# Mixing the Fourier modes with one product over all 128 rows for both halves of the row frequencies, factors padded with zeros, and the scratch tensor of the modes laid out anew

## The reference

```python
x_ft = jnp.fft.rfft2(x)
out_ft = out_ft.at[:, :, :MODES, :MODES].set(jnp.einsum('bixy,ioxy->boxy', x_ft[:, :, :MODES, :MODES], w1))
out_ft = out_ft.at[:, :, -MODES:, :MODES].set(jnp.einsum('bixy,ioxy->boxy', x_ft[:, :, -MODES:, :MODES], w2))
return jnp.fft.irfft2(out_ft, s=(h, w))
```

## Time and profile before

| | us |
|---|---|
| median of 3 runs | 3841.19 (3837.57 to 3843.26) |
| profiled execution, time | 3846.3 |
| profiled execution, span of the trace | 3844.5 |
| TensorE busy in the span | 3672.3 (96%) |
| VectorE busy | 3525.7 (92%) |
| ScalarE busy | 3397.2 (88%) |
| mean granted TensorE clock, share of full | 0.984 |

### The profile page before, as it was taken

One profiled execution on the slowest core, in us unless ns is written; L12 is line 12 of the kernel. 1 busy time (PEld: TensorE's weight loads), 2 busy tenths in 40 slices (PEclk: granted clock), 3 DMA queues, 4 the chain that ended last, 5 costly groups with the idle time before them and its releaser, 6 DMA issues.

```text
span 3844.5 us, 103434 instructions
## 1 busy us (share of the span) xinstructions
PE 3672.3 (96%) x38186; PEld 1791.6 (47%) x38186; DVE 3525.7 (92%) x3959; ACT 3397.2 (88%) x3512; POOL 110.8 (3%) x132
## 2 busy tenths in 40 slices
PE   4995679999999999999999999999999999999998
PEld 2443334444444444444444444444444444444444
DVE  5773269999999999999999999999999999999997
ACT  1551269999999999999999999999999999999996
POOL 0000000000000000000000000000000000000000
PEclk9996899999999999999999999999999999999999
DMA  5999542332233223222322332232223223322321
GB/s 144 290 284 181 172 117 60 71 71 62 62 71 71 58 67 71 65 60 70 71 64 60 71 71 59 65 71 69 58 68 71 65 59 71 71 61 63 71 71 45
DMA packets 327345, 328.77 MB, mean 86 GB/s; under 512 B 87040, under 2 KB 259584, under 8 KB 325248
## 3 DMA queue, kind: packets, MB, share of 16 engines
q1 hardware_dynamic: 304256, 256.74, 24.9%
q0 software_dynamic: 18432, 67.12, 10.8%
q10 hardware_dynamic: 4608, 4.20, 0.3%
HBM read 239.90 MB, written 88.08 MB: 85 GB/s over the span
## 4 chain that ended last, share of the span: by engine, by line
PE 85%; DVE 0%; issue 0%; ACT 0%; POOL 0%; POOLq 0%; ACTq 0%; DVEq 0%
PE l_ps L1068 80%; PE y_ps L1055 3%; PE y_ps L1047 2%; DVE cube2l L944 0%; DVE cube3r L944 0%; ACT above L983 0%; ACT size L994 0%; ACT offset L998 0%; ACT S L987 0%; ACT below L991 0%; DVE cube1r L944 0%; DVE cube1l L944 0%; DVE cube0l L944 0%; ACT L987 0%; DVE cube0r L944 0%
## 5 line engine op out<-in xcount | busy, mean ns | idle before, releaser
L998 ACT ACTIVATE offset<-size 128x1024 f32<-128x1024 f32 x1280 | 1240.4, 1044 | 8.1
L944 DVE SCALAR_TENSOR_TENSOR cube0r<-below,offset 128x1024 f32<-128x1024 f32 x256 | 312.4, 1220 | 57.6 <-ACT offset L998 57.0
L1068 PE MATMUL l_ps<-S,kan_w 64*64 64x512 f32 x2048 | 357.2, 591 | 7.9 <-issue 7.9
L1068 PE MATMUL l_ps<-cube1l,kan_w 64*64 64x512 f32 x2048 | 357.1, 589 | 1.3 <-issue 1.3
L1068 PE MATMUL l_ps<-cube3r,kan_w 64*64 64x512 f32 x2048 | 356.7, 589 | 0.9 <-DVE cube3r L944 0.9
L1068 PE MATMUL l_ps<-cube0r,kan_w 64*64 64x512 f32 x2048 | 356.7, 590 | 0.6 <-DVE cube0r L944 0.6
L1068 PE MATMUL l_ps<-below,kan_w 64*64 64x512 f32 x2048 | 357.0, 591 | 0.0
L1068 PE MATMUL l_ps<-cube3l,kan_w 64*64 64x512 f32 x2048 | 356.7, 589 | 0.1
L1068 PE MATMUL l_ps<-cube2l,kan_w 64*64 64x512 f32 x2048 | 356.7, 589 | 0.1
L1068 PE MATMUL l_ps<-cube4r,kan_w 64*64 64x512 f32 x2048 | 356.7, 589 | 0.1
L1068 PE MATMUL l_ps<-cube4l,kan_w 64*64 64x512 f32 x2048 | 356.7, 589 | 0.1
(11 more groups left out here) (126 smaller groups left out, 6832.8 us busy)
## 6 DMA issues: line engine op xcount, KB each, us to landing
big<-in_x_dram SPq DMA_DIRECT2D x128, 512.0 KB, 7.0
x_ring<-in_x_dram SPq DMA_DIRECT2D x256, 256.0 KB, 4.1
act_out<-in_x_dram POOLq DMA_DIRECT2D x128, 512.0 KB, 6.8
out_dram<-act_out SPq DMA_DIRECT2D x128, 512.0 KB, 2.7
rows_scratch<-rows SPq DMA_DIRECT2D x16, 1024.0 KB, 6.1
rows_t<-rows_scratch SPq DMA_DIRECT2D x512, 32.0 KB, 5.5
big<-in_spec_w_r_dram SPq DMA_DIRECT2D x16, 512.0 KB, 11.3
big<-in_spec_w_i_dram SPq DMA_DIRECT2D x16, 512.0 KB, 11.6
```

Of the source, the lines that this page charges most:

```text
L944: nc.vector.scalar_tensor_tensor(out=cube[q][side][:], in0=distance[layer][:], scalar=EDGE - KNOTS[q], in1=offset[layer][q][:], op0=ALU.mi ...
L998: nc.scalar.activation(offset[layer][q][:], size[layer][:], ACT.Square, bias=-KNOTS[q]).then_inc(offset_ready[layer], 1)
L1068: ins = nc.tensor.matmul(dst[cols, r * MM:(r + 1) * MM], kan_w[layer][rows_, f, :], src[rows_, n * MM:(n + 1) * MM], start=(f == 0), stop= ...
```

## The change

A product of the mixing now takes all 128 rows. Its stationary factor has 64 columns: 2 parts x 2 halves x 16 images. Where the column belongs to one half, the factor's rows of the other half are zero. The zeros come from the factors: `rs_own[:, half, :]` holds 1/sigma on the partitions of that half and zero on the others, `rs_neg` the same negated, and VectorE multiplies the modes by them, three multiplications of 512 elements per position. Two column frequencies (`col`) stand on the two 64-column halves of the array. `mixed` gets memory of its own. The modes' scratch tensor is laid out as place, part, half, image, column half, so that one row of `spec` is 4 KB in one piece, and the load per pair is two DMAs. The tables of the forward and inverse transforms are ordered to match (parts beside each other in place of in blocks), with the same sizes.

```diff
-MIX_M = 2 * B
-MIX_Q = MODES // 4
+MIX_Q = MODES // 2
...
-    modes_dram = nc.dram_tensor("modes_scratch", [2 * MODES, 4, 2, B, MIX_Q * C], F32, kind="Internal").ap()
+    modes_dram = nc.dram_tensor("modes_scratch", [MODES, 2, 2, B, 2, MIX_Q * C], F32, kind="Internal").ap()
...
-                            for col in range(4):
-                                for half in range(2):
-                                    ky, own = col * MIX_Q + at, slice(half * C, (half + 1) * C)
-                                    ins = nc.tensor.matmul(
-                                        ps[u][col * MIX_M:(col + 1) * MIX_M, half, at * C:(at + 1) * C],
-                                        normed[u][own, ky, 1 - part:3 - part, :].rearrange("p r b -> p (r b)"),
-                                        mix_w[g][part][own, :, x, ky], start=(part == 0), stop=(part == 1),
-                                        skip_group_check=True, tile_position=(half * C, col * MIX_M))
+                            for col in range(2):
+                                ky = col * MIX_Q + at
+                                ins = nc.tensor.matmul(
+                                    ps[u][col * C:(col + 1) * C, at * C:(at + 1) * C],
+                                    normed[u][:, ky, 1 - part:3 - part, :, :].rearrange("p f h b -> p (f h b)"), mix_w[g][part][:, :, x, ky],
+                                    start=(part == 0), stop=(part == 1), skip_group_check=True,
+                                    tile_position=(0, col * C))
...
-                        nc.scalar.activation(mixed[u], ps[u][:, :, 0:MIX_Q * C], ACT.Copy).then_inc(mix_kept, 1)
+                        nc.scalar.activation(mixed[u][:], ps[u][:], ACT.Copy).then_inc(mix_kept, 1)
...
-                        for half in range(2):
-                            n = x + (SH * half if g == 0 else 2 * MODES - SH * (half + 1))
-                            nc.scalar.dma_start(modes_dram[bass.ds(n, 1)].rearrange("n l r b f -> (n l r b) f"),
-                                                mixed[u][:, half, :]).then_inc(stored[u], 16)
+                        for col in range(2):
+                            dst = modes_dram[bass.ds(x + SH * g, 1), :, :, :, col, :]
+                            nc.scalar.dma_start(dst.rearrange("s r h b f -> (s r h b) f"),
+                                                mixed[u][col * C:(col + 1) * C, :]).then_inc(stored[u], 16)
...
+            nc.vector.memset(rs_own[:], 0.0).then_inc(rs_clear, 1)
+            nc.vector.memset(rs_neg[:], 0.0).then_inc(rs_clear, 1)
...
-            link(nc.vector.tensor_copy(rs_signed[:, 0, :], rs_c[:]))
-            link(nc.vector.tensor_scalar(rs_signed[:, 1, :], rs_c[:], -1.0, None, ALU.mult))
+            dve.wait_ge(rs_clear, 2)
+            for half in range(2):
+                own = slice(half * C, (half + 1) * C)
+                nc.vector.tensor_copy(rs_own[own, half, :], rs_c[own, :])
+                link(nc.vector.tensor_scalar(rs_neg[own, half, :], rs_c[own, :], -1.0, None, ALU.mult))
...
-                        nc.vector.tensor_tensor(
-                            normed[u][:, :, 1:3, :].rearrange("p k r b -> p r k b"), here,
-                            rs_signed[:, 0:1, :].unsqueeze(2).to_broadcast([P, 2, MODES, B]), ALU.mult)
-                        nc.vector.tensor_tensor(
-                            normed[u][:, :, 0:1, :].rearrange("p k r b -> p r k b"), here[:, 1:2],
-                            rs_signed[:, 1:2, :].unsqueeze(2).to_broadcast([P, 1, MODES, B]),
-                            ALU.mult).then_inc(normed_ready, 1)
+                        for f, part, scale in ((0, 1, rs_neg), (1, 0, rs_own), (2, 1, rs_own)):
+                            ins = nc.vector.tensor_tensor(
+                                normed[u][:, :, f, :, :], here[:, :, part:part + 1, :].to_broadcast([P, MODES, 2, B]),
+                                scale[:].unsqueeze(1).to_broadcast([P, MODES, 2, B]), ALU.mult)
+                        ins.then_inc(normed_ready, 1)
...
-                    for r in range(2):
-                        at = u * K + r * 2 * MODES
-                        sp.dma_start(spec[p][at:at + 2 * MODES, :].rearrange("n (l f) -> n l f", l=4),
-                                     modes_dram[:, :, r, bass.ds(2 * pair + u, 1), :].rearrange("n l b f -> n l (b f)"))\
-                          .then_inc(spec_loaded[p], 16)
+                    sp.dma_start(spec[p][u * K:(u + 1) * K, :],
+                                 modes_dram[:, :, :, bass.ds(2 * pair + u, 1)].rearrange("s r h b l f -> (s r h) (b l f)"))\
+                      .then_inc(spec_loaded[p], 16)
```

More of the change, by code:

```diff
@@ L123, in first_half @@
         big = sb("big", [P, 4, C * W])
-        rs_signed = sb("rs_signed", [P, 2, B])
+        rs_own = sb("rs_own", [P, 2, B])
+        rs_neg = sb("rs_neg", [P, 2, B])
         mix_loaded = [[ctx.enter_context(nc.semaphore(f"mix_loaded{g}{part}")) for part in range(2)] for g in range(2)]
-        t = dict(t, modes=modes, stats=stats, big=big, rs_signed=rs_signed, mix_loaded=mix_loaded)
+        t = dict(t, modes=modes, stats=stats, big=big, rs_own=rs_own, rs_neg=rs_neg, mix_loaded=mix_loaded)
         forward(nc, t)
@@ L489, in statistics_and_mix @@
 def statistics_and_mix(nc, t):
-    modes, stats, modes_dram, rs_signed, big = (t[n] for n in ("modes", "stats", "modes_dram", "rs_signed", "big"))
+    modes, stats, modes_dram, rs_own, rs_neg, big = (
+        t[n] for n in ("modes", "stats", "modes_dram", "rs_own", "rs_neg", "big"))
     conv_two, conv_bias, image_rs, pair_bias = t["conv_two"], t["conv_bias"], t["image_rs"], t["pair_bias"]
@@ L529, in statistics_and_mix @@
         var_ready, root_ready, chain = sem("var_ready"), sem("root_ready"), sem("chain")
-        rm_ready, bias_done = sem("rm_ready"), sem("bias_done")
+        rm_ready, bias_done, rs_clear = sem("rm_ready"), sem("bias_done"), sem("rs_clear")
         parts = big[:].rearrange("p i (o x k) -> p i o x k", x=SH, k=MODES)
         mix_w = [[parts[:, 2], parts[:, 3]], [parts[:, 0], parts[:, 1]]]
-        NRM, MXD = MODES * 3 * B, 2 * MIX_Q * C
+        NRM = MODES * 3 * 2 * B
         spare = stats[:].rearrange("p b g k -> p (b g k)")
-        normed = [spare[:, u * NRM:(u + 1) * NRM].rearrange("p (k r b) -> p k r b", r=3, b=B) for u in range(2)]
-        mixed = [spare[:, 2 * NRM + u * MXD:2 * NRM + (u + 1) * MXD].rearrange("p (h f) -> p h f", h=2)
-                 for u in range(2)]
-        ps = [ctx.enter_context(nc.psum_tensor(f"mix_ps{u}", [P, 2, MM], F32)) for u in range(2)]
+        normed = [spare[:, u * NRM:(u + 1) * NRM].rearrange("p (k f h b) -> p k f h b", f=3, h=2, b=B) for u in range(2)]
+        mixed = [sb(f"mixed{u}", [P, MIX_Q * C]) for u in range(2)]
+        ps = [ctx.enter_context(nc.psum_tensor(f"mix_ps{u}", [P, MIX_Q * C], F32)) for u in range(2)]
         normed_ready, mix_done, mix_kept = sem("normed_ready"), sem("mix_done"), sem("mix_kept")
@@ L677, in _ @@
                         dve.wait_ge(mix_done, 2 * x2 + (SH * g + u + 1))
[L678 to L685 removed]
+                        here = modes[:, bass.ds(place_, 1), g, :, :].rearrange("p s (k r) b -> p (s k) r b", r=2)
+                        for f, part, scale in ((0, 1, rs_neg), (1, 0, rs_own), (2, 1, rs_own)):
[3 more added lines that the diff above has]
+                        ins.then_inc(normed_ready, 1)
 def inverse_rows(nc, t):
@@ L764, in _ @@
                     pair = 2 * pair2 + p
-                    pe.wait_ge(spec_loaded[p], 64 * (pair2 + 1))
+                    pe.wait_ge(spec_loaded[p], 32 * (pair2 + 1))
                     for k in range(BANKS):
```

8 lines of the change are left out of this document (5 added, 3 removed).

## The result

| | before | after |
|---|---|---|
| median of 9 runs each, us | 3840.67 (3834.16 to 3844.44) | 3831.53 (3827.42 to 3834.39) |
| ratio, 95% interval | | 0.9977, 0.9968 to 0.9986 |
| profiled execution, span | 3844.5 | 3832.6 |
| mixing, first to last product | 344.11 to 415.70 | 344.18 to 403.65 |
| first product of the row stage | 425.55 | 414.07 |

The changed kernel is 9.1 us faster by the medians and 11.9 by the two traces. The forecast was 3809, 31.8 us less than before; the range began at 3799 and ended at 3831, half a microsecond too low. The direction was right, and so was the reading of the pauses as code; the price of a product and both terms of the row stage were not.

A forecast was written before the change was run, and what follows sets the result against it. It took instruction fetch to bound the mixing and waits for spec the row stage. Gains of 20.8 (mixing), 9.5 (row stage) and 1.5 (first loads), 31.8 us in all, took 3841.2 to 3809 us; range 3799 to 3831.

The forecast's parts named there:

- the reading of the pauses as code: Mixing: TensorE's 37.9 us of "issue" idle is waiting for the next block of 256 instructions; the change halves the blocks.
- the price of a product: Mixing: a 128-row, 64-column record takes 33 to 34 ns at full clock, 55 at half, as in the forward transform.
- Rivals 1 and 4: Mixing pauses: 1, they stay behind every block (6.6 us more, 3816, 10%); 4, they belong to positions (3831, 6%).
- Rival 4: Mixing: pauses are not code but belong to each position; 16 periods of 3.65 us stay, 3831 us, chance 6%.
- rival 5: Mixing: 64-column strips don't run side by side at half clock, streaming 512-byte steps at 112 ns; slower, 3873 us, chance 5%.
- Position 8 waits for its weights: Mixing: position 7 done at 373.4 us, position 8's weights landing at 374.9, so a new wait of 1.5 us.
- the forecast's late blocks: Mixing while weights load: code blocks executable only at 349.6 plus 6.7 us, then 7.6 each: 356.3, 363.9 and 371.5.
- Start: Mixing: extra VectorE work on factors and multiplications moves the first product from 344.1 to about 345.5 us.
- Rival 2: Mixing: the clock stays at half throughout, records at 55 ns to the end; 3817 us, chance 10%.
- Row stage, 9.5 us: Inverse along rows: fewer spec DMAs with 4 KB pieces cut waits from 3.0 to about 0.9 us; 9.5 us gained, bounds 3 and 13.
- first loads, 1.5: Start of row stage: two DMA issues in place of four shorten the 9.84 us first wait by 1.5, bounds 0.5 and 2.
- rival 3: Row stage gives nothing, since the stores' bytes set the chain; 9.5 us less gain, 3819 us, chance 8%.

The follow-up runs named there:

- e4: Kernel before, its 1024 mixing products written as two loops over pairs of positions, weights of two places only (for time alone): 3819.2 us, 20.8 less.
- e1: Changed kernel, positions 8 to 15 reading weights with steps of 1, 2, 8 and 32 elements in place of 128 (for time alone): 3831.72 us.
- e7: Changed kernel, all mixing weights read from contiguous 256-byte pieces, without the step (wrong weights, for time alone): 3823.81 us, 19.1 less than the kernel before.
- e5: Kernel before, positions 8 to 15 with other sets of 64-row tiles, or eight tiles without a step (for time alone): 3830.98 us.
- e2: Changed kernel, positions 8 to 15 with one or four strips, 32 moving or 32 stationary columns, step kept (for time alone): 3848.43 us.
- e3: Changed kernel, row stage issuing the spec loads of pair p+2 ahead of the stores of pair p: 3825.93 us, ratio 0.9962 to the kernel before.
- e6: Kernel before, spec loads of pair p+2 issued ahead of the stores of pair p, still 1 KB pieces: 3836.73 us, ratio 0.9984.

## Why the prediction was wrong, step by step

- **Pauses are code: right.** The 37.9 us of "issue" went, 8 packets came for 8 blocks, and e4, without any change to the tiles, shows no pause for code from the second pass on. Rivals 1 and 4 fall. Rival 4 named both the time, 3831, and the sign, a period of 3.65 us per 64 records, that then came; its cause was wrong all the same, and its time agrees by chance: 16 periods of 3.65 us are 58.4, some 13 less than the mixing took before, which its sum left out. The Trainium skill, "Runtime: NRT & Kernel Launch", Instruction fetch mechanics, calls the crossing mostly hidden; for these products it isn't: a block runs for 2.1 us and the next can be executed 3.65 us after it.
- **Price of a product: the term that failed.** The step was "the forward transform has just this shape (L434 ...) 33 ns each". The shape was the same, the layout wasn't: with a step of 512 bytes a record takes 56 ns (e1: 33 again by the same division at steps up to 8 bytes). The text named the difference, in rival 5, but allowed for it only at half clock. There it adds nothing (32 records in the same 1.70 us with the step and without); it counts at full clock, where it keeps a record at 56 while one without a step falls to 29. The upper bound given, "56 (no overlap)", was the value, by another cause. Mended for that alone (e7) the mixing ends at 394.2, where 394.9 was forecast. It cost 8.75 us of the 20.8: the mixing ended 12.05 us earlier.
- **Where the 12 us came from.** 64 records of 56 ns happen to equal the 3.65 us of one block, so in the quiet part nothing was gained. The whole gain lies in the stretch while the weights load, where a block took 7.6 us before.
- **The eight tiles.** The prediction set aside the rule on packing since runs of 2.1 us didn't show eight tiles of 7 ns. Behind the price of one tile with a step, the eight were there: 14.3 ns against 56 with two, 9.5 without a step (e5). The Trainium skill, "TensorEngine Tiling (Array Packing)", Theoretical Speedup, lets the number of tiles decide; the runs with a step agree from two to eight tiles, but for four tiles of full height (58 ns, e2).
- **Position 8 waits for its weights: didn't occur.** Positions took 3.6 us and position 8 was reached at about 375, with no wait in the trace.
- **A wait not in the sum:** ScalarE for its stores while the weights load, 20.1 us. The prediction had looked at their issue, 0.34 us each, and not at their landing, 6.8. It cost TensorE 1.6 us here and 7.6 in e7, where positions are short. There it took the place of the forecast's late blocks, so that e7's agreement before 375 is partly luck.
- **Start: nearly right.** TensorE's wait before the first product grew from 3.05 to 4.09 us, 1.0 where 1.4 was forecast. The rest is that the work ahead of it ended 1.0 us earlier in this execution.
- **Clock: of no weight.** It rose at about 347.5 us in place of 389, after TensorE had worked without a gap since 344.18. Rival 2's sign, records at 55 ns to the end, came, but not by the clock: it was at full from there on. (In the profile of the kernel before TensorE is under nine tenths in the first slice and in the fourth to sixth, and the granted clock is low in two slices, six tenths in the fourth and eight in the fifth, not as the text on the time before has it.)
- **Row stage, 9.5 us, and first loads, 1.5: wrong**, measured 0.1 and a loss of 0.6 (the wait grew from 9.84 to 10.42). The step was "the last is in the queue by 438 ... at 408 it is 1.3". Neither issue nor pieces set the wait (e3, e6); the 2.1 MB of stores ahead in the same queue do. The rate with 4 KB pieces was 270 GB/s, not 408. This is rival 3, at 8% too low. What spoke for it ("2 MB stand ahead of every spec") was a row; what spoke against it was a rate in a stretch that also has the end of the stores and the landing in it. Once the order is turned (e3), the stage takes 72.4 us from its first product to the next stage's, about what the forecast had, by another edit. For the first loads the step was the issue in an idle queue: from the first issue to the first product it took 4.95 us with four DMAs ahead (420.6 to 425.55) and 4.97 with two (409.10 to 414.07), so the number of issues set nothing; the rest of the loss is that the issues began later after the last product, and why isn't known.

The sum as it turned out: 12.05 from the mixing, -0.6 and 0.1 from the rows, 0.2 from an earlier start of the next stage: 11.8 of the 11.9 by which the spans differ. From the prediction's own start of 3841.2 that would be 3829.4, just inside the range; the medians of nine runs moved by 9.1 and not 11.9, and that scatter of the runs puts the result half a microsecond outside. The lesson is in the forecast itself: rivals 2 and 3 were each priced alone, and both came true in effect, as 3809 + 8 + 9.5 = 3827 would have said.

## What to carry to other kernels

The price of a matmul record is read from a line with the same layout as well as the same shape: a moving operand with a step of 32 bytes or more cost twice the array's time at full clock here, and the number of tiles at work divided it, but for four full-height tiles. When small written-out products show even pauses of "issue", count the instructions between them; fewer products or a loop remove them, but what the products themselves cost comes out only then. A short load that others wait for belongs ahead of large stores in a queue: that reordering took 9.9 us off the stage (e3) and 8.7 in the kernel before (e6), while larger pieces and fewer DMAs brought nothing.

## What had not been expected of the hardware

- A streamed operand of fp32 with a step of 32 bytes or more takes about 112 ns per 64 values and tile at full clock. With two tiles a record takes 59 ns at a granted clock of 0.50 and 56 at 1.00; with a step of up to 8 bytes it takes 29 to 31 at 1.00.
- Issuing one spec DMA takes SyncE 0.49 us ahead of two 1 MB stores and 1.11 behind them.
- With four full-height tiles at work (e2), an operation of VectorE that takes 0.69 us otherwise took 7.27, and a copy of ScalarE 5.67 in place of 0.60. The timelines of VectorE and ScalarE:

```profile
381.29 0.69 DVE L701 TENSOR_TENSOR stats<-modes,rs_neg 128x512 f32<-128x512 f32 x1 [5.20 <-PE mix_ps L599]
...
388.39 7.27 DVE L701 TENSOR_TENSOR stats<-modes,rs_neg 128x512 f32<-128x512 f32 x1 [5.21 <-PE mix_ps L599]
```

```profile
388.26 5.67 ACT L621 ACTIVATE mixed<-mix_ps 128x512 f32<-128x512 f32 x1 [6.44 <-PE mix_ps L599]
```

Four tiles of 64 rows had no such effect (e5: VectorE's operations are 0.69 us there too), nor had eight of them. That the streaming tiles simply read too much doesn't explain it: eight tiles of 64 rows at 14.3 ns a record draw 64 values per partition in 29 ns, four full-height ones only in 58. The cause stays open.
